# The mix as two 64-row matmuls per chunk in place of one block-diagonal matmul

## The reference, cut to what matters

```
W = weights[condition]                          # (64, 64, 64): one matrix per batch entry
y = einsum('bct,bcd->bdt', x, W)                # the mix: x is (64, 64, 1024)
w = (unpack(qweight) - zero_point) * scale      # (1024, 1024), six-bit values
out = x + einsum('bsk,nk->bsn', y, w) + bias    # the linear layer, then bias and residual
```

## Time and profile before

| | |
|---|---|
| median of 3 runs | 331.95 us (331.39 to 332.85) |
| span of the profiled execution | 331.5 us |
| its own time beside the span | the page gives none; the span itself lies inside the range of the runs |
| instructions | 5520 |
| TensorE matmul, busy | 319.6 us (96%), 1700 records |
| TensorE weight load, busy | 268.9 us (81%), 1700 records |
| VectorE, busy | 211.4 us (64%) |
| ScalarE, busy | 127.8 us (39%) |
| GpSimd, busy | 78.3 us (24%) |
| mean granted TensorE clock | 0.978 |
| DMA | 40.52 MB, mean 122 GB/s |

### The profile page before, as it was taken

One profiled execution on the slowest core, in us unless ns is written; L12 is line 12 of the kernel. 1 busy time (PEld: TensorE's weight loads), 2 busy tenths in 40 slices (PEclk: granted clock), 3 DMA queues, 4 the chain that ended last, 5 costly groups with the idle time before them and its releaser, 6 DMA issues.

```text
span 331.5 us, 5520 instructions
## 1 busy us (share of the span) xinstructions
PE 319.6 (96%) x1700; PEld 268.9 (81%) x1700; DVE 211.4 (64%) x262; ACT 127.8 (39%) x265; POOL 78.3 (24%) x39
## 2 busy tenths in 40 slices
PE   8797699999999999999999999999999999999995
PEld 3685588888888888888888888888888888888885
DVE  3459984666566676665666766656667666566563
ACT  4659157543333444433334444333344443330000
POOL 1006505222112222221122222211222222112000
PEclk9779599999999999999999999999999999999999
DMA  5895055625333333233333332433333321111112
GB/s 174 237 317 190 10 176 166 199 83 198 125 114 104 131 132 104 100 134 122 115 116 117 132 111 94 135 121 116 115 119 130 109 96 63 55 40 65 63 73 86
DMA packets 25805, 40.52 MB, mean 122 GB/s; under 512 B 11970, under 2 KB 12226, under 8 KB 25794
## 3 DMA queue, kind: packets, MB, share of 16 engines
q1 hardware_dynamic: 25794, 40.39, 36.5%
HBM read 23.59 MB, written 16.78 MB: 122 GB/s over the span
## 4 chain that ended last, share of the span: by engine, by line
PE 91%; DVE 3%; SPq 2%; DMA 1%; ACT 1%; issue 1%
PE o_ps L285 71%; PE y_ps L249 17%; PE ysum_ps L262 2%; DMA q_raw<-in_L_ffn_qweight_dram 1%; DVE q_bf L426 1%; DVE q_int L419 1%; DVE q_int L421 1%; ACT junk L346 1%; PE o_ps L270 1%; PE y_ps L285 1%; SPq L182 0%; SPq L148 0%; SPq L153 0%; SPq L144 0%; SPq L139 0%
## 5 line engine op out<-in xcount | busy, mean ns | idle before, releaser
L285 PE MATMUL o_ps<-qT,y_hi 128*128 128x512 f32 (+1 forms) x512 | 203.7, 399 | 0.0
L285 PE MATMUL o_ps<-qT,y_lo 128*128 128x512 f32 (+1 forms) x512 | 199.5, 390 | 0.0
L540 POOL TENSOR_TENSOR resid<-x_sb,bias_bc 128x1024 f32<-128x1024 f32 x32 | 77.1, 2414 | 221.6 <-DVE o_sb L462 195.7
L285 PEld LDWEIGHTS o_ps<-qT,y_hi 128*128 128x128 f32 x512 | 97.1, 190 | 20.0
L285 PEld LDWEIGHTS o_ps<-qT,y_lo 128*128 128x128 f32 x512 | 97.2, 190 | 19.1
L454 DVE TENSOR_TENSOR o_sb<-o_ps,scale_bc 128x512 f32<-128x512 f32 x63 | 43.6, 691 | 92.8 <-PE o_ps L285 92.8
L355 ACT ACTIVATE y_hi<-y_ps 128x512 fp32r<-128x512 f32 x64 | 38.2, 599 | 157.6 <-PE y_ps L249 157.6
L346 ACT ACTIVATE junk<-x_sb 64x1024 bf16<-64x1024 f32 x64 | 67.6, 1057 | 1.6
L249 PEld LDWEIGHTS y_ps<-w_sb,x_sb 128*128 128x128 f32 x512 | 63.6, 196 | 2.4
L249 PE MATMUL y_ps<-w_sb,x_sb 128*128 128x128 f32 x512 | 64.1, 280 | 0.0
L443 DVE SCALAR_TENSOR_TENSOR resid<-zs_bc,ysum,resid 128x1024 f32<-128x1024 f32 x32 | 60.4, 1886 | 0.0
(11 more groups left out here) (26 smaller groups left out, 45.3 us busy)
## 6 DMA issues: line engine op xcount, KB each, us to landing
x_sb<-in_x_dram SPq DMA_DIRECT2D x32, 512.0 KB, 3.3
out_dram<-o_sb SPq DMA_DIRECT2D x63, 256.0 KB, 2.0
q_raw<-in_L_ffn_qweight_dram SPq DMA_DIRECT2D x8, 384.0 KB, 5.4
w_sb<-in_L_cond_weights_dram SPq DMA_DIRECT2D x64, 16.0 KB, 2.0
w_stack<-in_L_cond_weights_dram SPq DMA_DIRECT2D x64, 16.0 KB, 2.1
scale_bc<-_L_ffn_weight_scale_dram SPq DMA_DIRECT2D x1, 512.0 KB, 6.1
zs_bc<-n_weight_zero_point_dram SPq DMA_DIRECT2D x1, 512.0 KB, 7.5
bias_bc<-in_L_ffn_bias_dram SPq DMA_DIRECT2D x1, 512.0 KB, 8.4
```

The lines of the kernel that those rows point to most:

```text
L285: last = nc.tensor.matmul(bank, part[:, slot, kt, :], qT[:, kt, col:col + width], start=(kt == 0 and part is y_hi), stop=(kt == KT - 1 and ...
L540: nc.gpsimd.tensor_tensor(resid[:, j % RING, :], x_sb[:, j % RING, :], bias_bc[:], ALU.add).then_inc(xbias_ready, 1)
```

## The change

mix issues two matmuls per chunk. Each takes 64 array rows (half 0: rows 0 to 63, half 1: rows 64 to 127) of the x chunk as its stationary operand, still 128 columns wide, and 64 columns of w_stack as its moving one. Half 0 and half 1 write different PSUM banks: y_ps is now [128, 2, 2, 8, 64], one bank per tile parity and batch entry, four banks as before. w_sb, its zeros, its DMAs and its semaphores are gone. y_ps_ready is signalled twice in the last chunk. high and low read one bank each and write 64-column pieces of every chunk of y_hi and y_lo, whose layout stays.

```
-        w_sb = sb("w_sb", [P, RING, P], F32)
-        y_ps = psum("y_ps", [P, 2, KT, P], F32)
+        y_ps = psum("y_ps", [P, 2, 2, KT, S], F32)
@@ last_pieces
-                       (y_ps[:, 0, 0:KT // 2, :].rearrange("p t r -> p (t r)")[:, 0:NH // 2], NH + NH // 2, NH // 2)]
+                       (y_ps[:, 0, 0, :, :].rearrange("p t r -> p (t r)")[:, 0:NH // 2], NH + NH // 2, NH // 2)]
@@ load_w
-                    sp.dma_start(w_sb[rows, j % RING, rows],
-                                 weights[bass.ds(picked[half], 1), :, :].rearrange("a c s -> (a c) s")
-                                 ).then_inc(w_loaded[j % RING], 16)
@@ start of the SyncE stream
-            sp.wait_ge(w_zeroed, 1)
@@ mix
-                pe.wait_ge(w_loaded[slot], (i + j // RING + 1) * 32)
+                pe.wait_ge(w_stacked[slot], (i + j // RING + 1) * 32)
                 for kt in range(KT):
-                    last = nc.tensor.matmul(y_ps[:, j % 2, kt, :], x_sb[:, slot, kt * P:(kt + 1) * P],
-                                            w_sb[:, slot, :], start=True, stop=True)
-                    if kt % (KT // 2) == KT // 2 - 1:
-                        last.then_inc(y_ps_ready, 1)
+                    for half in range(2):
+                        rows = slice(half * C, (half + 1) * C)
+                        last = nc.tensor.matmul(y_ps[:, j % 2, half, kt, :], x_sb[rows, slot, kt * P:(kt + 1) * P],
+                                                w_stack[rows, slot, :], start=True, stop=True)
+                        if kt == KT - 1:
+                            last.then_inc(y_ps_ready, 1)
@@ high
-                    chunks = slice(half * KT // 2, (half + 1) * KT // 2)
-                    nc.scalar.activation(y_hi[:, j % RING, chunks, :], y_ps[:, j % 2, chunks, :],
+                    cols = slice(half * S, (half + 1) * S)
+                    nc.scalar.activation(y_hi[:, j % RING, :, cols], y_ps[:, j % 2, half, :, :],
@@ low
-                    nc.vector.tensor_tensor(y_lo[:, j % RING, chunks, :], y_ps[:, j % 2, chunks, :],
-                                            y_hi[:, j % RING, chunks, :].bitcast(F32),
+                    nc.vector.tensor_tensor(y_lo[:, j % RING, :, cols], y_ps[:, j % 2, half, :, :],
+                                            y_hi[:, j % RING, :, cols].bitcast(F32),
@@ gpsimd
-            nc.gpsimd.memset(w_sb[:], 0.0).then_inc(w_zeroed, 1)
```

More of the change, by code:

```diff
@@ L93, in adaln_ffn @@
         last_pieces = [(o_ps[:, 1, 0:NH // 2], NH, NH // 2),
-                       (y_ps[:, 0, 0:KT // 2, :].rearrange("p t r -> p (t r)")[:, 0:NH // 2], NH + NH // 2, NH // 2)]
+                       (y_ps[:, 0, 0, :, :].rearrange("p t r -> p (t r)")[:, 0:NH // 2], NH + NH // 2, NH // 2)]
         ids_loaded = sem("ids_loaded")
         x_loaded = [sem(f"x_loaded{s}") for s in range(RING)]
-        w_loaded = [sem(f"w_loaded{s}") for s in range(RING)]
         w_stacked = [sem(f"w_stacked{s}") for s in range(RING)]
@@ L104, in adaln_ffn @@
         bias_loaded = sem("bias_loaded")
-        w_zeroed = sem("w_zeroed")
         xsum_zeroed = sem("xsum_zeroed")
@@ L147, in load_w @@
                     rows = slice(half * S, (half + 1) * S)
-                    sp.dma_start(w_sb[rows, j % RING, rows],
-                                 weights[bass.ds(picked[half], 1), :, :].rearrange("a c s -> (a c) s")
-                                 ).then_inc(w_loaded[j % RING], 16)
-                for half in range(2):
-                    rows = slice(half * S, (half + 1) * S)
                     sp.dma_start(w_stack[rows, j % RING, :],
```

## The result

The changed kernel takes 336.29 us (median of 4 runs, 335.26 to 338.5) against 332.4 us before in the same job (331.39 to 332.93): ratio 1.0131, 95% interval 1.0087 to 1.0175. It is slower, by 1.3%: a small loss, but clear of the noise. The forecast was 336.7.

A forecast was written before the change was run, and what follows sets the result against it. TensorE, busy 96% of the span, was taken to bound the kernel, so the mix's cost is unhidden. Span 331.5 + 0 (mix) + 6.0 (seams) - 1.3 (start) = 336.2, with 0.45 outside the span 336.7 us; range 331 to 393.

The forecast's parts named there:

- The loads of the two halves run beside each other: In the mix, loads for different array rows go in pairs, 16 double steps of 0.111 us, so it stays 1.78.
- The load sets the mix's pace: In the mix, a 128-column load takes about 0.105 us, already as long as the step, so halving the stream gains nothing.
- The seam: Shape change between linear and mix: 0.09 us of emptying plus 0.11 uncovered load, 0.20 in 30 mixes, 6.0 us.
- The start: SyncE's queue at the start loses two w_sb DMA issues, so q 3 lands earlier: 1.3 us gained.
- neither gain nor loss beyond the 1.36: At the start, GpSimd's additions and the VectorE unpacking they stretch both come earlier; counted as no further effect.
- the bound of -4.8: Largest start gain considered, if the shorter idle stretch also keeps TensorE's clock up; half speed was worth 3 to 3.4 us.
- The level: Whole kernel: median time taken as 0.45 us above the 331.5 us profiled span, turning 336.2 into 336.7.
- ScalarE, VectorE: ScalarE's first copy of y_ps starts 0.9 us later but stays hidden; copies are of the same 512 elements.
- A: Rival: the mix's loads come one by one, 1.77 us more per tile, 391.5 us; chance 0.28.
- B: Rival: half overlap in the mix, 3 load steps for 4, mix 2.66 us, together 364 us; chance 0.10.
- C: Rival: faster, the row split needs no emptying, seams cost 0, start's gain is left, 327.2 to 330.6 us; chance 0.10.
- D: Rival: as forecast, but the start's whole 4.8 us gain comes, 333.2 us, no measurable difference; chance 0.08.

The follow-up runs named there:

- half_stream: Kernel before, its mix streaming 64 columns in place of 128 against the same 128*128 operand, second batch entry's mix left out; 334.05 us, tile 9.42.
- same_rows_twice: Changed kernel with both matmuls of a chunk on array rows 0 to 63, first batch entry computed twice, second left out; 424.24 us.
- small_64_before_mix: Kernel before with one more small matmul, stationary operand w_stack 128*64, ahead of the mix of tiles 7 to 31; 341.73 us.
- sum_y through w_sb: Kernel before without w_stack and its DMAs, sum_y taking the 128*128 block-diagonal w_sb as stationary operand; 325.63 us, ratio 0.9802.
- halves_outside: Changed kernel with the mix's two loops exchanged: all 8 chunks of half 0, then all 8 of half 1; 400.87 us.
- changed_add_later: Changed kernel with a wait that keeps GpSimd's four additions behind the last unpacking; 335.64 us, ratio 1.0077.
- dmas_back_behind: Changed kernel with two idle DMAs per tile for the first four tiles, issued behind the w_stack ones; 337.96 us, ratio 1.0158.

## Why the prediction was right

- **The loads of the two halves run beside each other: right,** in steps of 0.111, and in keeping with the reason given: a load can pass a matmul that waits. The limit of about four pairs was not foreseen; the change's order of loops stays within it.
- **The load sets the mix's pace: right,** shown by half the stream (tile 9.42).
- **The seam: right in kind, too dear.** 0.20 was forecast, the tile shows 0.147. The 0.09 is there (the 0.32 less the 0.23). The likely reason for the missing 0.05, in the sum's terms: the change also halves the last stream of the mix, which nothing covers before the array empties into sum_y. half_stream, which has shorter streams and no new seam, is shorter by just 0.05 a tile. 30 x 0.147 = 4.4 in place of 6.0.
- **The start: too much was given back.** The seams less the measured differences leave 0 to 0.5 for it in place of 1.3. With GpSimd's additions held back in both kernels it is 1.3 (4.4 - 3.1), the forecast's figure, though by subtraction and within about 1 us. The prediction took the earlier additions as "neither gain nor loss beyond the 1.36"; the runs point to a loss of some 0.8 there, and that is not clear of the noise. The first low stretch of the clock did go with the longer queue, as the bound of -4.8 had it, but the changed kernel's clock falls later instead (from 23.9 and again from 34.1 us in one profile, from 31.7 in the other). Over a whole execution the two kernels have nearly the same mean clock, 0.985 to 0.99 in most timings of either, so the medians show little of that gain.
- **The level.** The prediction took the median as 0.45 above the span. In fact about 2 us lie around a span, and the profile of before was of a slow start. So in spans the forecast of 336.2 stands against 333.2 and 334.0 measured. That the forecast time is only 0.4 from the median is thus in part luck, for four errors nearly cancel: seams 1.6 too dear, the start's gain about 1 too large, a span of before that was 1.4 high for its median (331.95 - 1.8 = 330.15), and a distance from span to time taken 1.6 too small. The difference is the fairer measure: 4.75 forecast, 3.9 to 4.45 measured.
- **ScalarE, VectorE: right.** The copies wait for the end of the mix, and TensorE, busy for 86.58 of 86.58 us, waits for none of them.
- **The rivals.** A (single file) is what same_rows_twice does, and its price was mis-sized: 424.24 and not 391.5, since the clock falls too. Its time would have been outside the range. B did not occur: the pairs come 0.111 apart. C fell with the changed kernel's own tile, 9.62 and not 9.47: the seam is there for fewer rows, as it is for fewer columns in small_64_before_mix. Of D the first part came, full clock in the mix of tile 1, but not the gain of 4.8.

What stays open is the start. That the clock stays up over the mix of tile 1 goes with the shorter queue, in every profile of a kernel whose mix is not in single file. How much of the median that and the race of the unpacking are worth, each by itself, is not shown.

## What to carry to other kernels

Before halving what a matmul streams, price its load. Here the load of 128 columns took 0.11 us with 64 rows as with 128, as long as the step, and so splitting the rows bought nothing, even though both halves ran at once. Count the changes of the array's shape in a loop: here each cost about 0.09 us and uncovered a load, and a larger stationary operand with zeros in it (sum_y through w_sb) was cheaper than a small one of another shape. A single profile's start says little about a kernel's median: set its own time and mean clock beside those of the other executions, compare steady tiles by profile and starts by timings.

## What was not expected of the hardware

- Loads for different array rows start less than 10 ns apart and share a step of 0.111; they pair only over some four pairs of load and matmul (halves_outside gained 3.5 of 16 possible steps).
- The granted clock can fall with TensorE busy without a gap: 0.90 over 26.5 us in same_rows_twice, against 1.00 in the steady loops of before and of the changed kernel, and the linear step then takes 9.1 us in place of 7.48.
- A VectorE step of 1.22 us between two tensors in SBUF takes 3.31 beside a GpSimd addition (changed_add_later), and a step of the unpacking 2.1 to 2.7 in place of 0.5 (before, dmas_back_behind).
